# A graph and mixture-of-experts kernel: attention in 32 by 32 squares turned on VectorE, a scatter as straight code, and matmuls of zeros on TensorE

## The reference, cut to what matters

```python
x = x + _L0_gnn_ref(_layernorm(x), batch0, edge_index, edge_attr_16, ...)   # 32 graphs
x = x + _L0_ffn_ref(_layernorm(x)[None], ...)[0]
x = x + _L1_gnn_ref(_layernorm(x), edge_index, edge_weight, ...)
x = x + _L1_ffn_ref(_layernorm(x)[None], ...)[0]

# in _L0_gnn_ref, n = 16 nodes a graph, H = 8 heads of hd = 64
q, k, v = ((x @ W + b).reshape(num_graphs, n, H, hd) for W, b in ...)
attn = jnp.einsum('bnhd,bmhd->bnmh', q, k) * scale
attn = attn.at[b_idx, loc_src, loc_dst].add(edge_attr @ We + be)
attn = jax.nn.softmax(attn, axis=2)
out = jnp.einsum('bnmh,bmhd->bnhd', attn, v).reshape(n_total, hid)
return out @ Wo + bo
```

## Time and profile before

| | us |
|---|---|
| median of 3 runs | 785.2 |
| lowest, highest | 782.02, 785.22 |
| profiled execution | 785.76 |
| its span | 784.0 |

### The profile page before, as it was taken

One profiled execution on the slowest core, in us unless ns is written; L12 is line 12 of the kernel. 1 busy time (PEld: TensorE's weight loads), 2 busy tenths in 40 slices (PEclk: granted clock), 3 DMA queues, 4 the chain that ended last, 5 costly groups with the idle time before them and its releaser, 6 DMA issues.

```text
span 784.0 us, 22829 instructions
## 1 busy us (share of the span) xinstructions
PE 671.7 (86%) x8392; PEld 567.9 (72%) x8393; DVE 573.7 (73%) x1284; ACT 380.5 (49%) x676; POOL 120.1 (15%) x175
## 2 busy tenths in 40 slices
PE   2999979948488999999992599999399999999991
PEld 1458969944388999999982344444298999999991
DVE  4679959643789888889885563435768888888880
ACT  3430000031267777768764422220267888888880
POOL 2000000010000111423204100000010344233333
PEclk9899989979599999999996699999679999999996
DMA  9500111100147889898854730000137889989864
GB/s 310 221 1 3 43 44 43 43 2 13 59 155 269 285 291 328 289 303 293 289 178 96 288 108 1 0 1 1 70 114 235 264 261 270 256 273 273 262 204 87
DMA packets 37791, 127.93 MB, mean 163 GB/s; under 512 B 5440, under 2 KB 6032, under 8 KB 37568
## 3 DMA queue, kind: packets, MB, share of 16 engines
q1 hardware_dynamic: 31712, 119.39, 44.1%
q0 software_dynamic: 3648, 6.23, 5.5%
q10 hardware_dynamic: 2352, 1.23, 0.6%
HBM read 117.85 MB, written 10.03 MB: 163 GB/s over the span
## 4 chain that ended last, share of the span: by engine, by line
PE 68%; DVE 15%; issue 6%; DMA 3%; ACT 2%; POOL 2%; ACTq 1%; DVEq 1%; SPq 0%; POOLq 0%
PE pb L1487 12%; PE pb L1488 12%; PE pb L1489 12%; PE pb L1727 6%; PE pb L1588 6%; PE pb L1758 4%; PE pb L1760 4%; PE pb L1759 4%; DVE r_split L927 3%; DMA r_stage<-in_chunks 2%; PE pb L1587 2%; PE pb L1496 2%; PE pb L1586 2%; ACT r_split L680 1%; PE pb L1709 1%
## 5 line engine op out<-in xcount | busy, mean ns | idle before, releaser
L927 DVE SCALAR_TENSOR_TENSOR r_split<-r_stage,r_split 128x1024 f16<-128x1024 f32 (+1 forms) x160 | 230.5, 1442 | 47.7 <-ACT r_split L680 46.9
L680 ACT ACTIVATE r_split<-r_stage 128x1024 f16<-128x1024 f32 (+1 forms) x160 | 197.3, 1236 | 49.4 <-PE pb L1760 31.3
L1487 PE MATMUL pb<-r_work,r_split 128*128 128x160 f16 x864 | 184.1, 234 | 8.2 <-DVE r_work L1347 6.4
L1489 PE MATMUL pb<-r_work,r_split 128*128 128x160 f16 x864 | 184.1, 234 | 0.0
L1488 PE MATMUL pb<-r_work,r_split 128*128 128x160 f16 x864 | 184.1, 234 | 0.0
L1758 PE MATMUL pb<-r_work,r_split 128*128 128x160 f16 x608 | 131.0, 234 | 5.2 <-ACT r_work L754 2.8
L1760 PE MATMUL pb<-r_work,r_split 128*128 128x160 f16 x608 | 131.1, 234 | 0.0
L1759 PE MATMUL pb<-r_work,r_split 128*128 128x160 f16 x608 | 131.0, 234 | 0.0
L1487 PEld LDWEIGHTS pb<-r_work,r_split 128*128 128x128 f16 x864 | 84.8, 98 | 10.3 <-issue 6.2
L1586 PE MATMUL pb<-r_work 128*128 128x64 f16 x512 | 87.7, 195 | 3.7 <-DVE r_work L1054 3.7
L1587 PE MATMUL pb<-r_work 128*128 128x64 f16 x512 | 87.5, 196 | 2.0 <-issue 2.0
(11 more groups left out here) (281 smaller groups left out, 1263.9 us busy)
## 6 DMA issues: line engine op xcount, KB each, us to landing
r_stage<-in_chunks SPq DMA_DIRECT2D x68, 768.0 KB, 5.7
r_stage<-in_chunks SPq DMA_DIRECT2D x92, 512.0 KB, 4.7
r_gnn<-in_cheb_lin SPq DMA_DIRECT2D x3, 1024.0 KB, 9.2
r_split<-in_cheb_lin SPq DMA_DIRECT2D x3, 1024.0 KB, 12.5
x_dram<-x_sb SPq DMA_DIRECT2D x10, 256.0 KB, 2.8
x_sb<-in_x SPq DMA_DIRECT2D x1, 1024.0 KB, 5.7
r_split<-in_Wq SPq DMA_DIRECT2D x1, 1024.0 KB, 9.6
r_work<-in_attr SPq DMA_DIRECT2D x1, 1024.0 KB, 10.8
```

The lines of the kernel that those rows point to most:

```text
L680: nc.scalar.activation(x.hi(c), x.stage(c), ACT.Copy, scale=W_SCALE).then_inc(x.whi, 1)
L927: V.scalar_tensor_tensor(x.lo(c), x.stage(c), W_SCALE, x.hi(c), ALU.mult, ALU.subtract)\
L1487: MM(o, sh, mh, start=start, stop=False)
L1489: return MM(o, sl, mh, start=False, stop=stop)
```

## The change

The scatter of the narrow case is written out, all 32 batches. Attention keeps pairs of graphs as 32 by 32 squares: DVE multiplies the exponentials by share and mask into 128 x 256 for each t, and turns each square by `V.transpose` within its 32 partitions; PE multiplies 32 rows by 32 columns, four quarters q for each t, a quarter after the one before has ended. The softmax goes in three groups of t. All tiles have buffers and banks of their own. The quarters of t = 2 and 3 lie between the matmuls of `project` 0 and 1. PE multiplies zeros in three places. The statistics of three rows go between the last additions, the scales and `diag` under the power, and PE's `diag` matmuls behind the router.

```diff
-        prob = [view(r_work, 4 * b, H * P, F32, "p (h j k) -> p h j k", h=H, j=GP) for b in range(2)]
-        probT = [view(r_work, 8 + 4 * b, H * P, F32, "p (h q) -> p h q", h=H) for b in range(2)]
+        GROUPS = ((0, 1), (1, 2), (2, T))
+        prob = [view(r_work, t, H * 32, F32) for t in range(T)]
+        probT = [view(r_work, 4 + t, H * 32, F32, "p (h n) -> p h n", h=H) for t in range(T)]
...
+            edge_sums(0)
+            exponents(0)
+            edge_sums(1)
+            exponents(1)
+            edge_sums(2)
+            edge_sums(3)
+            exponents(2)
+            for t in range(T):
+                head_out(t)
...
-            def layernorm(n, dst, again=False):
+            def layernorm(n, dst, again=False, done=0, meanwhile=None):
...
-                for t in range(T - 1):
+                for t in range(done, T - 1):
                     ch.add(V.bn_stats(stats[:, t, :], x_sb[:, t, :]))
...
                 V.tensor_scalar(var_eps[:, :], mv[:, :, 1], LN_EPS, None, ALU.add).then_inc(var_ready, 1)
+                if meanwhile:
+                    meanwhile()
                 dve.wait_ge(rstd_ready, n + 1)
...
+            def logits(g):
+                a, b = GROUPS[g]
+                eb = pb[6 + a // 2][:, :].rearrange("p (t s q) -> p t s q", t=2, s=2)[:, a % 2:a % 2 + b - a, :, :]
+                for s in range(2):
+                    ch.link(V.scalar_tensor_tensor(flat[:, a:b, :], eb[:, :, s, :], 1.0 / EB_SCALE, flat[:, a:b, :],
+                                                   ALU.mult, ALU.add))
+                ch.link(V.tensor_reduce(hmax[:, a:b, :], score[:, a:b, :, :], AX_X, ALU.max))
+                V.tensor_tensor(score[:, a:b, :, :], score[:, a:b, :, :], bc(hmax[:, a:b, :], 3, GN), ALU.subtract)\
+                    .then_inc(logits_ready, 1)
...
+            def turned(t):
+
+                ch.link(V.tensor_tensor(prob[t].rearrange("p (h g k) -> p h g k", h=H, g=2), bc(score[:, t, :, :], 2, 2),
+                                        bc(share_of[:, t, :, :], 3, GN), ALU.mult))
+                V.transpose(probT[t].rearrange("p h n -> p (h n)"), prob[t]).then_inc(probT_ready, 1)
...
+            logits(0)
+            logits(1)
+            normalizers(0)
+            turned(0)
+            logits(2)
+            normalizers(1)
+            turned(1)
+            head_lo(0)
+            normalizers(2)
+            turned(2)
+            head_lo(1)
+            turned(3)
+            degrees()
+            head_lo(2)
+            project(0)
+            head_lo(3)
+            project(1)
+            row_stats(0)
+            project(2)
+            row_stats(1)
+            row_stats(2)
+            project(3)
             dve.wait_ge(x1_ready, T)
-            layernorm(1, xn)
+            layernorm(1, xn, done=T - 1, meanwhile=scales)
...
             def narrow_scatter():
-                turns = 8
-                with pe.Fori(0, C // (2 * GC * turns)) as i:
-                    firsts = window_starts(i * (2 * GC * turns))
-                    for r in range(turns):
-                        coming = []
...
+                firsts = window_starts(0)
+                rounds = C // (2 * GC)
+                for r in range(rounds):
+                    coming = []
...
-            def attend(t):
-                pe.wait_ge(probT_ready, 2 * (t + 1))
...
+            def attend(t, q):
+
+                pe.wait_ge(probT_ready, t + 1)
+                if q == 0:
+                    pe.wait_ge(adj_ready, t + 1)
+                else:
+                    pe.wait_ge(o_psum, 4 * t + q)
+                rows_q = slice(32 * q, 32 * q + 32)
                 for h in range(H):
...
+                    c = (h // 2) * P + 32 * q
+                    last = MM(pb[t][HD * (h % 2):HD * (h % 2) + HD, c:c + 32],
+                              v_sb[rows_q, t, h * HD:(h + 1) * HD], probT[t][rows_q, h, :], start=True, stop=True)
                 last.then_inc(o_psum, 1)
...
+            def keep_busy(bank, n):
+
+                for _ in range(n):
+                    MM(pb[bank][:, :], zeros[:, :], iota_n[:, :], start=True, stop=True)
+
+            keep_busy(4, 14)
+            pe.wait_ge(qw_lo, 4)
+            for t in range(2):
+                for q in range(4):
+                    attend(t, q)
+            for t in range(T):
                 for k in range(K):
...
+                    if t < 2:
+                        attend(t + 2, k)
+                    project(t, k)
...
+            keep_busy(1, 12)
             transpose_x(1)
             x_split(1)
             pe.wait_ge(x1_ready, T)
             route(0)
+            for t in range(T):
+                pe.wait_ge(diag_ready, t + 1)
+                MM(pb[3][:, t * P:(t + 1) * P], ones[:, :], diag[:, t, :], start=True, stop=True)\
+                    .then_inc(dinv_psum, 1)
+            keep_busy(1, 14)
             positions(0)
             experts(0)
```

More of the change, by code:

```diff
@@ L1109, in _ @@
             flat = score.rearrange("p t h k -> p t (h k)")
[L1110 to L1117, removed]
@@ L1148, in _ @@
[L1148 to L1159, removed]
@@ L1160, in _, with row_stats, degrees @@
-            for t in range(T):
-                V.tensor_scalar(diag[:, t, :], ident[:, :], dinv[:, t:t + 1], None, ALU.mult).then_inc(diag_ready, 1)
+                V.scalar_tensor_tensor(x_sb[:, t, :], pb[4 + t][:, :], XW_BACK, x_sb[:, t, :], ALU.mult, ALU.add)\
+                    .then_inc(x1_ready, 1)
+            def row_stats(t):
+                dve.wait_ge(x1_ready, t + 1)
+                ch.add(V.bn_stats(stats[:, t, :], x_sb[:, t, :]))
+            def degrees():
+                dve.wait_ge(adj_ready, T)
+                ch.link(V.tensor_scalar(has[:, :], deg[:, :], 0.0, None, ALU.is_gt))
+                ch.link(V.tensor_tensor(deg[:, :], deg[:, :], has[:, :], ALU.mult))
+                ch.link(V.scalar_tensor_tensor(deg[:, :], has[:, :], -1.0, deg[:, :], ALU.mult, ALU.add))
+                V.tensor_scalar(deg[:, :], deg[:, :], 1.0, None, ALU.add).then_inc(deg_ready, 1)
@@ L1642, in attend @@
-            def attend(t):
-                pe.wait_ge(probT_ready, 2 * (t + 1))
-                if t < 2:
-                    pe.wait_ge(adj_ready, T)
-                else:
-                    pe.wait_ge(ohi_ready, t - 1)
-                    pe.wait_ge(olo_ready, t - 1)
-                for h in range(H):
-                    o = pb[t % 2][HD * (h % 2):HD * (h % 2) + HD, (h // 2) * P:(h // 2 + 1) * P]
-                    last = MM(o, v_sb[:, t, h * HD:(h + 1) * HD], probT[t % 2][:, h, :], start=True, stop=True)
-                last.then_inc(o_psum, 1)
@@ L1674, in _ @@
+            keep_busy(4, 14)
[4 more added lines that the diff above has]
+            for t in range(T):
+                for k in range(K):
+                    if t < 2:
+                        attend(t + 2, k)
+                    project(t, k)
             pe.wait_ge(x1_ready, T)
-            for t in range(T):
-                pe.wait_ge(diag_ready, t + 1)
-                MM(pb[3][:, t * P:(t + 1) * P], ones[:, :], diag[:, t, :], start=True, stop=True)\
-                    .then_inc(dinv_psum, 1)
```

118 lines of the change are left out of this document (43 added, 75 removed).

## The result

| | before | after |
|---|---|---|
| median, us | 785.21 | 773.95 |
| lowest, highest (4 runs each) | 782.02, 785.82 | 772.3, 776.33 |
| profiled execution | 785.76 | 772.6 |

The account below looks back on a forecast made before the run. PE was taken as the scatter's bound and nearly full behind the gather; scatter 8.2, attention 10.0, LayerNorm 2.6 and turns 0.6 sum to 21.4 off 785.76, giving 764.4. Own range 761 to 768; 8 in 10, 758 to 771.

Parts of the forecast that it names:

- The scatter: PE's scatter loop: straight code removes the half-way jump, 5.5 us of standing and 2.7 of half clock, gain 8.2 us.
- so I expect the clock to fall between S+5.5 and S+9 and to return only some 3 to 5 us after the dense stretch begins at S+10.1: PE's clock in attention, S being the release of `scatter_psum`: half of 4.5 us lost, 2.3, leaving a gain of 10.0.
- the kind of work: Attention on PE: small f32 parts resemble the earlier window after which the clock fell; argument against the zeros holding full clock.
- full clock: Rival, chance 0.25: zeros hold PE's clock throughout, attention gains 12.3, total gain 25.1, time 760.5 us.
- An `attend` part: Attention on PE: eight f32 matmuls, 0.3 us near L1571's row, 0.5 with the wait; over 0.7 would be wrong.
- the S+23.8 of the sum: Attention: x ready 23.8 us after the release of `scatter_psum` at full clock, against S+36.1 before, gain 12.3 us.
- short matmuls are dear: Rival on attention: 32 rows cost like 128 columns, 1.4 us a part with wait; 773 us; dear matmuls or turns 0.12.
- half-way case: Milder form of the dear-matmuls rival (0.12): parts at 0.5 and 0.7 us, 2 to 3 us more, 767.
- LayerNorm: From x ready to the first turn on PE: 3.2 us instead of 5.8, gain 2.6.
- Turns and last zeros: Behind LayerNorm: the 16 turns at full clock gain 0.6 us; the last 14 zeros before the gather are booked at 0.
- The gap: Rival, chance 0.07: PE's stand at the scatter's middle has another reason and stays, 8.2 us less gain, 772 us.
- jump of the expert loops: Rival "slower", chance 0.03: moved PE code makes expert loops' jumps dear, 8.2 us each; all six give 813 us.

## Why the prediction was wrong

**The scatter: right.** 7.7 us of 8.2, the jump and its half clock gone, PE still the bound; alone 7.9 by the trace and 8.8 by the median.

**Attention: the step that failed** is "so I expect the clock to fall between S+5.5 and S+9 and to return only some 3 to 5 us after the dense stretch begins at S+10.1". The first half held (S+8.3). The second took any dense stretch for a stretch that brings the clock back. Where 2.3 us were booked, the half clock cost 9.8: eight units at 2.39 instead of 1.33 us are 8.5, and six more matmuls of the projection (180.50 to 182.99) at 0.427 instead of 0.215 are 1.3. The kernel with two zeros between and 14 ahead gives the same by another way: its x came 7.2 us sooner (S+29.9), though its eight pairs of zeros take 0.32 us each, 2.6 in all. With the squares put first the clock was back 3.4 us after the last of them, and with wide zeros in their place under 4 us into the mix. The text had the argument in hand: it gave "the kind of work" as the reason against full clock, and then did not apply it to the mix, two thirds of whose time at full clock I had in wide matmuls. It should have been a rival of its own.

**Attention: a term that was mis-sized.** An `attend` part was priced at 0.5 alone and 0.3 in the mix. It is 0.80 and 0.69 at full clock; the first is over the "0.7 us" that the text named as a sign of being wrong. L1571 with 11 ns a record was the wrong neighbour, and not only for the wait at the end of each quarter: inside a quarter, where nothing is waited for, the first 4 records take 0.30 us, the first 8 0.42 and all 16 0.65, so about 29 ns a record. L1571 has weights of 64 rows and 32 columns, the quarters of 32 rows and 64 columns (`64*32` and `32*64` in the rows); whether that is the reason was not tried. Eight quarters by 0.39 are 3.1 us in the mix, and eight by 0.3 are 2.4 before it, of which a part lay in PE's idle time. In the kernels that held the clock x came at S+29.9 and S+30.1; less the 2.6 of their pairs of zeros that is S+27.3 at best, 3.5 us behind the S+23.8 of the sum. So the rival "full clock" was too cheap too: with 8.8 for attention and the measured terms up to the first hidden matmul it is about 765, not 760.5. The rival "short matmuls are dear", half-way case (0.5 and 0.7), came nearest to this part and had the time wrong, 767, since it kept the forecast's clock.

**LayerNorm: right**, 2.7 for 2.6, with 3.11 us from x to the first turn where 3.2 was written; the terms given for it add up to 3.06.

**Turns and last zeros: right within a microsecond.** 1.4 together for 0.6 and 0. From the first turn to the router 0.9 us were gained. The lower clock was there when the 14 zeros started, as the text held likely; they did delay the positions, by 0.8 us, and bought 1.3 in the gather: 0.5 gained where 0 was booked.

**The rest of the span** shrank by 2.5 us, which no step held. It varies from 562.7 to 567.1 between the kernels of this study that compute all of the output; its cause stays open, and it should not be put down to the change.

**The other rivals.** The gap did not stay. No jump of the expert loops became dear (241 ns at most).

**A version that beats both** is the changed kernel with two zero matmuls behind each quarter of t = 0 and 1: 765.45 us, ratio 0.9751 [0.9709, 0.9792] to the kernel before, against 0.9867 [0.9826, 0.9908].

## What to carry to other kernels

Before counting on PE's full clock in a dense stretch, look at what fills it: find in the trace a stretch of the same kind of matmul that rose, not merely one that was full. Where small matmuls can't be avoided, it pays to keep the clock up ahead of them, and it may pay to put them all first, though two of the four executions of that kernel came at 772.6 and 775.2 us. With eight heads the mix here never brought the clock back, and the lower clock cost 10 us. Price short matmuls by a row of the same shape, weights included, and with the same waits, and write out a loop only where the row of its own jump shows the stall.

## What the runs showed of the hardware that was not expected

- PE 100% busy for 18 us (20 us without zeros) with the granted clock at 0.50, in a mix of 32-row f32 matmuls and wide f16 ones. With 1.00 on entry the same mix held 1.00 for 10 us in two kernels; in one execution of a third, with another order, it was lost 1.2 us in.
- Two 512-column matmuls of zeros behind each 0.65 us quarter held the clock, one did not, though PE was no less busy with one (2.99 of 3.00 us against 2.92).
- The same kernel came out at 762.4 and at 775.8 us in different executions with the mix one t earlier, and at 767.2 and at 775.2 with the squares first; the mean granted clock was lower in the longer ones (.946 against .963, .939 against .950).
- Records of 32-row f32 matmuls with 32 columns are 29 ns apart at full clock, those of 64 rows and 32 columns of L1571 11 ns.
- A branch of PE's sequencer ahead of the spare turns of the experts (`eng.If(n > 0)`), untouched by the change, takes as long as the jump that was removed. In the changed kernel:
```profile
L450 PEldq COMPARE_BRANCH  x2: 80/1844/3607, 399.4 to 696.8; - x2
```
One of its two takes 3.6 us, the other 0.08 (in the kernel before 3.3 and 0.08), and no run here says why, nor what it costs the span.
